# First batch's context transposes moved ahead of the last normalisation's transposes in a four-layer attention kernel

## The reference, cut to what matters

```
h = LN(x, g1, be1);  x = attn(h, h, wq1, wk1, wv1, wo1) + bo1 + x     # 20 heads, 56 keys
h = LN(x, g2, be2)                                                   # the "last normalisation"
q = h @ wq2;  k = ctx @ wk2;  v = ctx @ wv2                          # ctx: 1500 rows of 96
x = softmax(q k^T * scale) v @ wo2 + bo2 + x                         # 20 heads (8 in the third block)
x = geglu(LN(x, g3, be3)) + x
```

## Time and profile before

| | |
|---|---|
| median of 3 runs | 6827.93 us |
| profiled execution | 6827.41 us, span 6825.6 us |
| TensorE matmul busy | 6130.0 us (90% of the span) |
| ScalarE, GpSimd, VectorE busy | 3119.6, 3025.1, 2825.0 us |
| granted TensorE clock, mean | 0.896 |

### The profile page before, as it was taken

One profiled execution on the slowest core, in us unless ns is written; L12 is line 12 of the kernel. 1 busy time (PEld: TensorE's weight loads), 2 busy tenths in 40 slices (PEclk: granted clock), 3 DMA queues, 4 the chain that ended last, 5 costly groups with the idle time before them and its releaser, 6 DMA issues.

```text
span 6825.6 us, 106957 instructions
## 1 busy us (share of the span) xinstructions
PE 6130.0 (90%) x34384; PEld 5012.1 (73%) x34384; DVE 2825.0 (41%) x4978; ACT 3119.6 (46%) x7280; POOL 3025.1 (44%) x2992
## 2 busy tenths in 40 slices
PE   7999999999999999988888888999888998989998
PEld 5777777777777777766666666777777777777776
DVE  1444344443443444324454542544444444444442
ACT  1444444444444444444444442544454444444444
POOL 0444444444444444434444442544444444444444
PEclk8899899899898899888999996888898888888888
DMA  2000000000000000001011101000000000000000
GB/s 49 15 14 14 10 14 14 14 14 14 14 12 14 14 14 14 18 9 26 22 29 24 26 24 24 17 14 14 14 14 14 14 17 14 14 14 14 18 13 9
DMA packets 84450, 114.90 MB, mean 17 GB/s; under 512 B 42814, under 2 KB 64682, under 8 KB 83978
## 3 DMA queue, kind: packets, MB, share of 16 engines
q1 hardware_dynamic: 83978, 108.56, 5.7%
HBM read 104.06 MB, written 4.46 MB: 16 GB/s over the span
## 4 chain that ended last, share of the span: by engine, by line
PE 67%; issue 10%; DVE 9%; ACT 7%; POOL 5%; DMA 2%; ACTq 0%; POOLq 0%; DVEq 0%; SPq 0%
PE ps_c L667 15%; PE ps_c L1043 6%; PE ps_u L1116 6%; PE ps_s L1101 5%; PE ps_s L1103 5%; PE ps_s L1102 5%; PE ps_u L1117 5%; PE ps_u L1118 5%; POOL p_lo L1569 4%; PE ps_c L1062 3%; ACT p_hi L1782 2%; PE ps_c L1025 1%; PE ps_c L845 1%; DMA w_area<-recs 1%; PE ps_c L871 1%
## 5 line engine op out<-in xcount | busy, mean ns | idle before, releaser
L1569 POOL TENSOR_TENSOR p_lo<-p,p_hi 125x448 fp32r<-125x448 f32 (+2 forms) x2688 | 2721.0, 1022 | 2999.2 <-ACT p_hi L1782 2813.5
L1780 ACT ACTIVATE p<-ps_s 125x448 f32<-125x448 f32 (+2 forms) x2688 | 1320.7, 491 | 2286.6 <-PE ps_s L1103 2056.8
L1419 DVE TENSOR_REDUCE mpiece<-ps_c 125x1 f32<-125x500 f32 (+1 forms) x1984 | 1267.5, 672 | 292.9 <-PE ps_c L1043 272.8
L1782 ACT ACTIVATE p_hi<-ps_s 125x448 fp32r<-125x448 f32 (+2 forms) x2688 | 1315.7, 489 | 0.0
L1101 PE MATMUL ps_s<-q_hi,ctxT_hi 105*125 105x448 f32 (+3 forms) x2688 | 1033.0, 384 | 161.7 <-issue 84.4
L1116 PE MATMUL ps_u<-p_hi,ctx_hi 125*97 125x448 f32 (+2 forms) x2688 | 1028.8, 383 | 127.0 <-POOL p_lo L1569 122.3
L1102 PE MATMUL ps_s<-q_lo,ctxT_hi 96*125 96x448 f32 (+2 forms) x2688 | 957.7, 356 | 0.0
L1103 PE MATMUL ps_s<-q_hi,ctxT_lo 96*125 96x448 f32 (+2 forms) x2688 | 954.8, 355 | 0.0
L1117 PE MATMUL ps_u<-p_hi,ctx_lo 125*96 125x448 f32 (+2 forms) x2688 | 948.1, 353 | 0.0
L1118 PE MATMUL ps_u<-p_lo,ctx_hi 125*97 125x448 f32 (+2 forms) x2688 | 946.8, 352 | 0.0
L1043 PE MATMUL ps_c<-ctxT_hi,q_hi 96*125 96x500 f32 (+1 forms) x2112 | 865.0, 421 | 67.3 <-DVE ctxT_lo L1403 34.6
(11 more groups left out here) (231 smaller groups left out, 6026.6 us busy)
## 6 DMA issues: line engine op xcount, KB each, us to landing
ctx_raw<-in_ctx SPq DMA_DIRECT2D x96, 562.5 KB
pT<-recs SPq DMA_DIRECT2D x32, 420.0 KB, 3.3
w_area<-recs SPq DMA_DIRECT2D x32, 420.0 KB, 3.4
w_area<-recs SPq DMA_DIRECT2D x32, 168.0 KB, 3.6
cs<-in_ctx SPq DMA_DIRECT2D x192, 6.0 KB, 2.8
x_between<-x_out SPq DMA_DIRECT2D x32, 80.0 KB
x_in<-x_between SPq DMA_DIRECT2D x32, 80.0 KB
w_area<-in_L_xattn_wq SPq DMA_DIRECT2D x2, 800.0 KB, 5.7
```

The source lines that it names most:

```text
L1419: z = V.tensor_reduce(mpiece[0:wide, k, r:r + 1], C(0, wide, n % banks(t), 0, PIECE), AX.X, ALU.max)
L1569: P.tensor_tensor(p_lo[0:kp, k % 3, 0:w], p32[0:kp, k % 2, 0:w], p_hi[0:kp, k % 3, 0:w].bitcast(F32), ALU.subtract).then_inc(*sig("pl_ready"))
L1780: A(p32[0:kp, k % 2, 0:w], ps_s[0:kp, k % 2, 0:w], ACT.Exp, scale=DH[t.ph] ** -0.5)
L1782: A(p_hi[0:kp, k % 3, 0:w], ps_s[0:kp, k % 2, 0:w], ACT.Exp, scale=DH[t.ph] ** -0.5)\
```

## The change

The parts in the second half's lane are put in another order. `pre` of the next pair is cut once more, at the step named in `LAST_NORM`: what lies after it (on TensorE step 39 in phase 0 and 19 in phase 2, the transposes of `xn`; on ScalarE the step that writes `hT`) follows the context part. On VectorE and GpSimd the normalisation's own steps lie before the cut (38 and 18), so there the context part comes after them. New order: rest of `pre`, `context` of batch element 0, the normalisation's transposes, `queries`, `maxima`. In phase 1 nothing is cut, and `context` and `queries` change places. The waits are adapted: the context's first transposes wait for the attention's add (`xm_ready`), the transposes of `xn` wait for `ctl_ready` (`ctxT_lo` of the bank that they reuse: the second in phase 0, the first in phase 2), the queries for the third `ctxT_lo`, and the maxima for the last `q_lo`.

```diff
+        LAST_NORM = (38, None, 18)
...
-            def before(t, b):
-                return [part("split", side.split, t) if b else part("queries", side.queries, t),
-                        part("context", side.context, t, b), part("maxima", side.maxima, t, b)]
+            def before(t, pre=None):
+
+                if pre is None:
+                    return [part("split", side.split, t), part("context", side.context, t, 1),
+                            part("maxima", side.maxima, t, 1)]
+                head, norm = [pre], []
+                if t.ph != 1:
+                    rest, norm = cut(*pre, LAST_NORM[t.ph])
+                    head, norm = [rest], [norm]
+                return head + [part("context", side.context, t, 0)] + norm + [part("queries", side.queries, t),
+                                                                              part("maxima", side.maxima, t, 0)]
...
-                    parts, tail = [pre_b] + before(t + 1, 0), TAIL
+                    parts, tail = before(t + 1, pre_b), TAIL
...
                 def norm(t, n, bank):
 
+                    if n and not t.ahead:
+                        pe.wait_ge(*got("ctl_ready", t, bank + 1))
                     pe.wait_ge(*got("xn_ready", t, n + 1))
...
-                            pe.wait_ge(*got("xm_ready", t, per("xm_ready", t)))
+                            pe.wait_ge(*got("ctl_ready", t, NPIECE))
                             if t.ph != 1:
                                 pe.wait_ge(*got("ht_ready", t, 2))
...
                             if b == 0:
-                                pe.wait_ge(*got("ql_ready", t, per("qs_ready", t)))
+                                pe.wait_ge(*got("xm_ready", t, per("xm_ready", t)))
...
-                            if n == 0 and b:
-                                pe.wait_ge(*got("ql_ready", t, per("ql_ready", t)))
+                            if n == 0:
+                                pe.wait_ge(*got("ql_ready", t, per("ql_ready" if b else "qs_ready", t)))
```

More of the change, by code:

```diff
@@ L498, in pair @@
                 norm = [] if first else [apart(side.normalise(t + (-1), 1))]
-                parts = before(t, 1)
+                parts = before(t)
                 end = [] if first else [part("post", side.post, t + (-1))]
@@ L520, in schedule @@
                 t = At(ph, 0)
-                weave(iter(()), lane(([] if ph else [part("pre", side.pre, t, first=True)]) + before(t, 0)))
+                if ph:
+                    begin = [part("context", side.context, t, 0), part("queries", side.queries, t),
+                             part("maxima", side.maxima, t, 0)]
+                else:
+                    begin = before(t, part("pre", side.pre, t, first=True))
+                weave(iter(()), lane(begin))
                 pair(t, first=True)
@@ L996, in queries @@
                         if g == 0:
-                            pe.wait_ge(*got("xm_ready", t, per("xm_ready", t)))
+                            pe.wait_ge(*got("ctl_ready", t, NPIECE))
                             if t.ph != 1:
                                 pe.wait_ge(*got("ht_ready", t, 2))
-                            else:
-                                pe.wait_ge(*got("mr_ready", t, 0))
                         if g >= banks(t):
@@ L1019, in context @@
                             if b == 0:
-                                pe.wait_ge(*got("ql_ready", t, per("qs_ready", t)))
+                                pe.wait_ge(*got("xm_ready", t, per("xm_ready", t)))
+                                if t.ph == 1:
+                                    pe.wait_ge(*got("mr_ready", t, 0))
+                                if t.ph == 2 and isinstance(t.it, int) and t.it == 0:
+                                    pe.wait_ge(*got("ht_ready", t, 2))
                         if r >= banks(t):
```

## The result

| | before | after |
|---|---|---|
| median of 20 runs each | 6828.77 us | 6750.17 us |
| profiled execution | 6827.41 us | 6721.46 us |
| granted TensorE clock, mean | 0.896 | 0.913 |

The ratio is 0.9905, 95% interval [0.9881, 0.9929]: 1% faster. 6854 us had been forecast, with a range of 6785 to 6920 us. Ratios here leave out the runs that took over 1.5% longer than the fastest of the same kernel (beside e5 to e8 that leaves only 7 of 21 runs of the kernel before, since one of them took 6728.94 us), so they can differ from the quotient of two medians.

What follows compares the result with a forecast made beforehand. TensorE's chain was taken to bound the kernel, through its waits and its clock. From the profiled 6827.4 us, 21 + 32 + 3 - 25 - 4 = +27 gave 6854 us, range 6785 to 6920 us.

Steps and rivals of the forecast that it cites:

- What bounds the kernel: TensorE's chain: its waits, and as larger stake its clock in the queries, 10.6 us a phase 0 pair, 8.2 in phase 2.
- Phase 0's waits: New waits ahead of phase 0's queries, first query 4.4 us later: net +1.4 us a pair, +21 us over 15 pairs.
- Phase 0's clock: Phase 0's queries at the low clock in all 15 pairs instead of 12: 3 x 10.6 = +32 us.
- Phase 2's waits: Ahead of phase 2's queries: wait of about 2.4 us, first query 3.6 us later, net +0.2 us a pair, +3 us.
- Phase 2's clock: Phase 2's queries at the low clock in 10 of 15 pairs instead of 13: 3 x 8.2 = -25 us.
- the second rival: Phase 2's queries keep the full clock thanks to the denser stretch ahead of them: 6773 us, chance 0.12.
- the forecast of -4 us: Phase 1's waits at context transposes, queries and maxima: 2.25 us instead of 1.11 + 1.38, -4 us over 15 pairs.
- The transposes: Context transposes leaving the low-clock stretch behind the queries: taken as 0, between -1.2 and +1.2 us each, -30 to +30 us.

Runs made afterwards that it cites:

- e5: The kernel before, order untouched, with 7 unread matmuls of 448 columns in phase 2's wait for `hT` ahead of the queries: 6713.14 us, ratio 0.9899.
- e8: The changed kernel with VectorE's context ahead of `xn` (phases 0 and 2) and GpSimd's `ctx_lo` two `p_lo` later in phase 0: 6670.59 us, ratio 0.9851.
- e2: The change in phase 0 only, phases 1 and 2 in the order of the kernel before: 6873.58 us, ratio 1.01.
- e12: The changed kernel, but in phase 2 the first 24 queries come directly behind the `xn` transposes, the tiles after them: 6856.91 us, ratio 1.0026.
- e3: The change in phase 1 only, phases 0 and 2 in the order of the kernel before: 6822.96 us, ratio 1.0002.
- e11: Another order than the changed kernel's: last normalisation with its transposes first, then context transposes, then queries; no matmul added: 6546.22 us, ratio 0.9556.
- e4: The kernel before, order untouched, with 26 unread matmuls of 64 columns in phase 2 between `xn` transposes and queries: 6855.48 us, ratio 1.0034.
- e6: The changed kernel, but VectorE makes `ctx_hi` and the three `ctxT_lo` ahead of `xn` in phases 0 and 2: 6701.49 us, ratio 0.9875.
- e7: The changed kernel, but GpSimd makes `ctx_lo` of phase 0 two `p_lo` later: 6768.08 us, ratio 0.9973.

## Why the prediction was wrong

**What bounds the kernel: right.** It named the clock in the queries as the larger stake, and its prices, 10.6 and 8.2 us a pair, hold: over all loop pairs of the kernel before, a low one is 10.4 us longer in phase 0 and 8.0 in phase 2, and the 11 pairs of phase 2's stretch that came back are 90 of the 97 us measured.

**Phase 0's waits: right in kind, too dear.** Forecast 2.0 us for `ctxT_lo` and about 1.5 for `hT`, measured 1.62 and 0.97 to 1.29, with 0.91 for `p_lo` between them; the queries 4.4 us later, measured 9.45 - 5.53 = 3.9. TensorE's waits in the first of the four stretches grew from 206.3 to 217.1 us, by 11 and not by 21.

**Phase 0's clock: right in count, 15 of 15.** With 53 us forecast for both terms, the profile shows 24 and e2's medians 49 (its own profile 19), so the size is known only to within that.

**Phase 2's waits: right.** No wait at `xn`, 2.2 us for `p_lo` ahead of it (2.4 forecast), queries 3.5 us later (3.6 forecast).

**Phase 2's clock: the step that failed.** "I take 10 of 15 instead of 13", worth -25 us; it was 1 of 15, about -98. I had written down both facts that decide it, that the wait is "with 2 us of dense matmuls behind it, before the queries", and that a clock that has fallen "stays low until the queries are done", and then sized the count by the *length* of the wait. What counts is what TensorE does next. Behind tiles a fall cost 3.4 us at half clock, among queries it lasts past their end. e5 and e12 show it from either side: same order with full clock, same wait with low clock. It was the second rival, "phase 2 keeps the clock", 6773 us at a chance of 0.12, that came true.

With the measured 12 pairs in place of 3 the sum is 21 + 32 + 3 - 98 - 4 = -46, or 6781 us. That lies 31 us above the measured median, and the largest part of the rest in the profile is phase 0, 53 forecast and 24 measured.

**Phase 1: the forecast of -4 us stands** within e3's interval; its waits are those forecast.

**The transposes** leaving the low stretch, taken at 0, were not measured apart. A low pair of phase 0 takes 181.9 us after and 182.3 before in the mean, though its waits grew by 0.7 us, so some 1 us a pair may come from there, near the lower end of the range given; no run shows that it does. Nor does any run show whether transposes alone hold or raise the clock, the rule of the Trainium skill ("TensorE: Matmul & The Clock Gate", Part 4: PE-mode transpose) that the prediction weighed: in the change and in e11 they are mixed with tiles. That stays open.

## What to carry to other kernels

Where the granted clock has two levels, ask of each wait not how long it is but what comes behind it: put matmuls that bring the clock back (here tiles of 448 columns) between a wait and a long stretch that doesn't (here 40 queries of 128 columns on 80 rows). Why the queries don't is not known: their width, their rows and their data type were not varied one by one. Before reordering anything, fill the suspected wait with dense matmuls that nobody reads; as long as they fit into the wait they delay nothing (in e5 the first query kept its place, in e4 it came 1.07 us late), and they say what the clock is worth there. A sum of waits that grows while the time falls is a sign that the clock is the matter; the page's mean clock says it directly, since (1 - clock) times the span is an estimate of what the low level costs: 710 us before, 585 after.

## What the runs showed of the hardware that I had not expected

- TensorE busy for 15.00 of 15.00 us with the queries and a few tiles' matmuls among them stays at the low level, and the queries at the high level keep it (both in the earlier trace rows). Whether a fall lands there decides some 8 to 11 us a pair. The level at the first query does not: it was high in all 13 low pairs of the old phase 2, and in two pairs of phase 2 after the change (from 5142.2 and 6217.4) the first queries ran at 0.50 and the clock was back 1.7 us later.
- Matmuls of 64 columns with a new 125-column weight each came every 0.106 us, and 2.76 us of them did not keep the clock from falling; seven of 448 columns, one every 0.2 us, held it.
- `xn` on VectorE (128x160, f32) took 0.36 us with GpSimd idle, 0.69 us when `p_lo` ran beside it, 1.65 us beside `ctx_lo`: each time it ended 0.1 us after the GpSimd instruction that was running when it began, and so did all 272 such `xn` in the traces of before, after, e6, e7 and e8. `ctxT_lo`, beside the same `ctx_lo`, was not lengthened (1.26 us for two in e6, as in e8). The Trainium skill ("GPSIMD Engine Reference", 1. Specifications) says that the two engines share their SBUF interfaces, with contention when the VectorE instruction is in a two-port mode or has two inputs in SBUF. The trace agrees that they contend, and shows the rest of the GpSimd instruction as the price; which of the two conditions `xn` meets no run shows.
